# Edge rows loaded ten tiles at a time into a ring of three places, in a graph kernel that sorts its edges

## What is computed

```
edge_proj = edge_attr @ W_sum + b_sum
sum3d = segment_sum(edge_proj, src, num_segments=num_nodes)
cent_term = sigmoid(centralities @ W_cent + b_cent)
vor_term = sigmoid(voronoi_values @ W_vor + b_vor)
ref = h + z_in[in_deg] + z_out[out_deg] + cent_term + vor_term + sum3d
h = maximum(layernorm(x), 0);   result = x + ref
```

## Time and profile before

| | us |
|---|---|
| median of 3 runs | 2478.27 |
| span of the profiled execution | 3079.2 |
| POOL busy in it | 1853.9 (60%) |
| DVE busy | 1683.0 (55%) |
| PE busy | 1621.7 (53%) |
| ACT busy | 819.8 (27%) |

### The profile page before, as it was taken

The page is one execution under the profiler, slowest core; times in us unless marked ns, Lnnn a source line. Parts: engine busy times, 40 slices in busy tenths (PEclk is TensorE's granted clock), DMA queues, the critical chain, the costliest instruction groups (busy, mean ns, idle before and its releaser), DMA issues.

```text
span 3079.2 us, 40112 instructions
## 1 busy us (share of the span) xinstructions
PE 1621.7 (53%) x8689; PEld 1230.9 (40%) x8689; DVE 1683.0 (55%) x5737; ACT 819.8 (27%) x4073; POOL 1853.9 (60%) x1869
## 2 busy tenths in 40 slices
PE   5644555455555432226555554444456665568766
PEld 1223444344333320014444444333355554456655
DVE  7554456666666631346656654333455554468866
ACT  3312222232322332442232322222222222200323
POOL 5556665556565667665555655656655555556676
PEclk7756666666666655557767777767777777789988
DMA  4245433334444443334555555555556666579896
GB/s 122 85 127 151 116 106 107 99 104 122 122 121 121 126 135 106 88 107 137 155 152 164 160 160 161 143 151 148 155 156 181 183 187 178 169 189 231 210 248 187
DMA packets 485070, 451.89 MB, mean 147 GB/s; under 512 B 72407, under 2 KB 444637, under 8 KB 484828
## 3 DMA queue, kind: packets, MB, share of 16 engines
q1 hardware_dynamic: 402782, 300.08, 37.0%
q0 software_dynamic: 78752, 136.44, 14.1%
q10 hardware_dynamic: 3294, 12.80, 1.3%
HBM read 319.28 MB, written 129.59 MB: 146 GB/s over the span
## 4 chain that ended last, share of the span: by engine, by line
another core or an unknown queue 34%; DVE 19%; PE 17%; issue 15%; ACT 7%; DMA 3%; SPq 2%; POOL 2%; DVEq 1%; ACTq 0%; POOLq 0%
PE bank L1001 8%; ACT junk L864 6%; DVE hot_dh L605 3%; DVE hot_n L670 3%; DVE acc L697 2%; DVE hot_dl L605 2%; PE bank L949 2%; POOL sorted L513 2%; DMA edge_ring<-in_L_gnn_z_out_dram,out_i 2%; SPq L408 2%; DVE gate_normed L736 2%; PE bank L984 1%; PE bank L1026 1%; DVE hot_t L605 1%
## 5 line engine op out<-in xcount | busy, mean ns | idle before, releaser
L513 POOL DMA_INDIRECT sorted<-edge_ring,pos_i x1660 | 1605.8, 967 | 1103.1 <-DVE pos_i L799 633.4
L1001 PE MATMUL bank<-piece_ring,hot_n 128*125 128x129 f32 x4920 | 885.4, 336 | 260.0 <-DVE hot_n L670 209.0
L864 ACT ACTIVATE junk<-bank,mark_col 128x100 bf16<-128x100 f32 x1664 | 550.4, 343 | 1748.6 <-remote 1221.3
L1001 PEld LDWEIGHTS bank<-piece_ring,hot_n 128*125 128x125 f32 x4920 | 823.2, 241 | 367.0 <-DVE hot_n L670 248.7
L697 DVE TENSOR_TENSOR acc<-bank,acc 125x129 f32 x1230 | 352.8, 287 | 698.6 <-remote 523.9
L984 PE MATMUL bank<-hot_w,after_b 128*128 128x400 bf16 x416 | 189.3, 455 | 806.1 <-ACT junk L864 560.7
L670 DVE SCALAR_TENSOR_TENSOR hot_n<-bank,wkey,piece_ring 128x250 f32<-128x250 f32 x1230 | 579.9, 472 | 11.8 <-issue 5.2
L984 PEld LDWEIGHTS bank<-hot_w,after_b 128*128 128x128 bf16 x416 | 49.5, 119 | 866.8 <-ACT junk L864 594.3
L864 ACT ACTIVATION_READ_ACCUMULATOR junk<-bank,mark_col 128x1 f32 x1664 | 338.1, 203 | 12.3 <-issue 12.3
L605 DVE TENSOR_TENSOR hot_dl<-dst_parts,bank 128x400 bf16<-128x400 bf16 x416 | 148.0, 356 | 337.1 <-remote 305.5
L1026 PE MATMUL bank<-hot_dl,hot_dh 128*125 128x100 bf16 x1661 | 207.2, 276 | 237.4 <-DVE hot_dh L605 197.6
(11 more groups left out here) (109 smaller groups left out, 1183.2 us busy)
## 6 DMA issues: line engine op xcount, KB each, us to landing
piece_ring<-sorted SPq DMA_DIRECT2D x1230, 130.0 KB
edge_ring<-in_edge_attr_dram SPq DMA_DIRECT2D x332, 320.0 KB
sorted<-edge_ring,pos_i POOLq DMA_INDIRECT x1660
base<-in_x_dram SPq DMA_DIRECT2D x20, 560.0 KB
out_dram<-base ACTq DMA_DIRECT2D x19, 560.0 KB
out_dram<-base SPq DMA_DIRECT2D x9, 560.0 KB
base<-out_dram SPq DMA_DIRECT2D x9, 560.0 KB
edge_ring<-in_L_gnn_z_out_dram,out_i POOLq DMA_INDIRECT x100
```

Of the source, the lines that this page charges most:

```text
L513: g.indirect_dma_start(rows, bass.IndirectOffsetOnAxis(index, 0), edge_ring[:, slot, at, :], None).then_inc(s_scatter[slot], 16)
L864: last = a.activation(junk[:, t, :], part[:, t // 2, :, t % 2], ACT.Relu, bias=mark_col[:, :], accum_out=pos_f[:, q % 4, t:t + 1])
L1001: last = t_.matmul(to, hot_n[:, n % HOT_SLOTS, k, :], piece_ring[:, n % PIECE_SLOTS, k, 0:SUM], start=(k == 0), stop=(k == ROW_GROUPS[s] - 1))
```

## The change

Two numbers change:

```diff
-LOAD_TILES = 5
-EDGE_SLOTS = 6
+LOAD_TILES = 10
+EDGE_SLOTS = 3
```

## The result

The kernel with ten tiles a load took 2498.68 us, the median of 4 runs (2495.39 to 2503.53); the kernel before took 2479.23 in 4 runs beside it. The ratio is 1.0073, with a 95% interval from 1.006 to 1.0086. So the change costs 18 us by the ratio and 19.5 by these two medians. The forecast of no change (2479.5) did not come. The time lies inside the stated range (2472 to 2510) only because that range allowed for the first rival, "the smaller cushion shows" (2490, up to 2511), to which the prediction gave a chance of 0.25.

What follows compares the result with a forecast made beforehand. POOL's 1660 scatters at 1.266 us each were taken to bound the kernel, other engines running ahead; every term was 0 except 0 to 3 us on 2478.3, taken as 2479.5 us, range 2472 to 2510.

Steps and rivals of the forecast that it cites:

- the smaller cushion shows: Rival, chance 0.25: quads 25 to 31, 216, 346 outrun the cushion or quads 347 to 394 lag POOL; 5 to 33 us.
- POOL sets the pace: Whole run: 1660 scatters, one each 1.266 us, bound the kernel; the other engines run ahead; chance 0.62, with cushion sufficing.
- The tail: After the last scatter starts: 368.0 us in the profile, a little shorter in the measured runs.
- Fewer instructions, the start: ACT loses 166 row keys, SP 166 issues; longer first loads at the start stay hidden, 5 us to spare: 0 us.
- A load must wait for more of the ring: Edge ring: POOL has 20 tiles in hand, not 25; cushion falls from 24.9 to 17.0 us, still enough: 0 us.
- The load behind the third piece: Quads 347 to 394: edge load issued behind that wait costs the chain 2.1 us each; POOL loses 0 to 3 us.
- passes 5.9 us: Quads 347 to 394: the landing time of a load that decides whether the smaller-cushion rival holds.
- the prediction's own formula: Chain time per ten tiles, quads 347 to 394: 2.5q plus L + 4.5 - 2q + 0.35, quad time q, load L.
- Its own sign of being wrong: Whole run: a median over 2483 with longer ACT waits for loads, meaning a cushion under 17 us or never filled.
- Heavy quads: Quads 31, 216 and 346: making lists holds DVE 7 to 11 us over normal; the 17 us cushion covers one.
- The stops are real in the runs as well: Rival, chance 0.05: POOL waits on the chain in measured runs too, each load costs; 60 to 140 us, say 2570.
- Larger transfers help: Rival, chance 0.08 (faster): POOL's scatter issue is held up less by SP's; 8.3 us, so 2470 us.

Runs made afterwards that it cites:

- e4: Kernel before, using five of its six edge-ring places (20 tiles in hand, as in the changed kernel) with LOAD_AHEAD 3 for 4: 2481.09 us, ratio 0.9999.
- e11: Changed kernel, with half the bytes in the piece loads of quads 345 to 396, all but the first twelve: 2494.3 us, ratio 1.0047 to the kernel before.
- e2: Changed kernel, with each ten-tile edge load one quad earlier in SP's list (LOAD_AHEAD 3 for 4): 2483.59 us, ratio 1.0005 to the kernel before.
- e6: Changed kernel, with only the edge loads of quads 214 and 344 moved two quads earlier in SP's list: 2494.6 us, ratio 1.0058 to the kernel before.

## Why the prediction was right and wrong, step by step

*POOL sets the pace: right.* Step, counts and first scatter stayed. The stops of the profile of before belonged to that execution, as assumed: the new profile of before has 38.8 us of waiting for indices where the earlier trace rows have 633.4.

*The tail: right in kind, too long in the sum.* 368.0 us by the earlier trace rows, 348.4 in the new profile. The prediction saw that it had to be shorter, from 2491.7 against 2478.27.

*Fewer instructions, the start: right, 0 us.* The first scatter starts at 21.9 us in after.

*A load must wait for more of the ring: right, 0 us.* e4 takes this alone and measures 0.9999. The cushion in steady quads can be read as the time from the end of a cast to its quad's first scatter. Its median over quads 60 to 330 was 22.0 us in before, 17.6 in after and 16.5 in e4, where the sum had 24.9 for before and 17.0 for after.

*The load behind the third piece: the step that failed.* The prediction had the mechanism, the quads and the threshold ("11.7 us, while POOL takes 12.66"; "passes 5.9 us"), and put its cost at 0 to 3 us. It cost some 16.5. Three of its terms missed: two made the loop's time too short, and the cushion was taken as too full.

First, the load. It was taken at 5.0 us from issue to row key, and the median of the whole program in after is 5.1; but in quads 347 to 394 it was 6.2, from 4.8 to 7.3. Put into the prediction's own formula, with a quad of 3.85 us: 0.5 x 3.85 + 6.2 + 4.85 = 13.0 us. That alone passes 12.66. The traffic beside it explains most of it: with less of it the load took 5.4 (e11) and 5.1 (e2). By the fit in "DMA: Bandwidth & Descriptors" of the Trainium skill, anatomy of one DMA, which is for a transfer on the POOL path, an estimate is 3.5 us. The trace does not agree: it has 5.1 and 6.2. Here is what the engines did while the load of 1842.58 was under way, and behind it (columns as above; 0.94 and 0.52 are PE's granted clock, 0.96 and 0.33 the DMA share, 287 and 74 GB/s):

```profile
1842.60:1850.00 7.40, 2.84 (x25) 2.50 (x22) 5.62 (x20) 0.15 (x2) 5.11 (x6) 0.94 0.96 287
1852.10:1856.00 3.90, 3.90 (x20) 3.90 (x19) 1.65 (x7) 1.41 (x8) 2.98 (x4) 0.52 0.33 74
```

The prediction bounded the load at 3.4 and 6.8 from rows where 231 GB/s were moved, and took a value near the middle. The right stretch to price it from was the burst in which it is issued, 287 GB/s here and 278 on average over the 20 loads.

Second, the third piece. The prediction put its end 2.15 us behind the start of `rank`, by taking three fifths of the time of five pieces. The granted clock was 0.78 over its 3.85 us, so part of it ran at the higher level. But the quad that counts is the one that follows PE's wait for the load. PE in after:

```profile
1843.07 2.37 PE L1001 MATMUL bank<-piece_ring,hot_n 128*125 128x129 f32 x20
1851.42 0.51 PE L984 MATMUL bank<-hot_w,after_b 128*128 128x400 bf16 x1 [5.98 <-ACT junk L864]
...
1852.40 4.07 PE L1001 MATMUL bank<-piece_ring,hot_n 128*125 128x129 f32 x20
```

After 5.98 us without work, `rebase` takes 0.51 us in place of 0.33 and five pieces take 4.07 in place of 2.37; the granted clock is 0.52 in the row above, so the lower of its two levels (1.2 GHz). From `rank` at 1852.06 to the end of the third piece at 1852.60 + 2.59 = 1855.19 it is 3.1 us, 1.0 more than taken. So the wait makes the next load later, which makes the next wait. What the clock adds of the 13.45 us was not tried by itself. The quads between run faster than the 3.85 us taken, 2.7 from 1840.18 to 1842.90, and that gives back part. In all, issue to row key is 6.04 us on average over the 19 intervals, 1.0 more than taken, and the rest of the loop is 7.41 us in place of 0.5 x 3.85 + 4.85 = 6.78, so 0.6 more: 11.78 + 1.04 + 0.63 = 13.45.

Third, the cushion at the entry. The prediction let 15 us of it absorb the loss in these quads. But quads 343 to 345 empty it: the index of quad 342 was ready 21.7 us ahead of POOL, that of quad 345 0.3 us. SP's list at the start of the last segment in after:

```profile
1748.75 0.39 SPq L421 DMA_DIRECT2D edge_ring<-in_edge_attr_dram  x1
1761.93 6.02 SPq L408 DMA_DIRECT2D piece_ring<-sorted  x10
1768.01 0.42 SPq L421 DMA_DIRECT2D edge_ring<-in_edge_attr_dram  x1
1768.62 22.08 SPq L408 DMA_DIRECT2D piece_ring<-sorted  x15
1790.76 0.42 SPq L421 DMA_DIRECT2D edge_ring<-in_edge_attr_dram  x1
```

Before the first piece of a sorted segment, SP waits until all of its tiles are scattered (12.2 us in after, 11.9 in before), then issues ten piece loads in one go, and only then the edge load: 1768.01 - 1748.75 = 19.3 us between two edge loads, and 22.8 us to the next. In before there are five piece loads ahead of the first edge load and five between it and the next:

```profile
1758.80 2.89 SPq L408 DMA_DIRECT2D piece_ring<-sorted  x5
1761.74 0.42 SPq L421 DMA_DIRECT2D edge_ring<-in_edge_attr_dram  x1
1762.36 2.87 SPq L408 DMA_DIRECT2D piece_ring<-sorted  x5
1765.28 0.43 SPq L421 DMA_DIRECT2D edge_ring<-in_edge_attr_dram  x1
```

At quad 345 the index was ready 4.8 us ahead of POOL's first scatter in before and 0.3 us in after. Before then gains on POOL and is at 12 us by quad 350. After stays between 0.3 and 4.4 us up to quad 396. The place of the edge load is the smaller part of this: with the load moved ahead of SP's wait (e6) the index of quad 345 is ready 4.1 us ahead, and in e2, which loses nothing, 1.6. The wait for the whole segment stands in all of these runs; only a loop slower than POOL fails to fill the cushion again behind it. So nothing was left to absorb 20 x (13.45 - 12.66) = 16 us, and 16.5 were measured. The sum of the prediction had this loss at 18 us in its worst case and took 15 off for the cushion. Its own sign of being wrong named this: a median over 2483, since the cushion was smaller "or never filled".

*Heavy quads, taken as covered: 4 us too small.* Around quad 216 POOL waited 5.3 - 1.2 = 4.1 us longer than in before, and no longer once the load of quad 214 was moved (e6). The rest of quads 217 to 339 cost nothing, as predicted: the first scatter of quad 235 starts 3.9 us later than in before, that of quad 340 3.5. The 4.1 us were of the same kind as at quad 345: an edge load late in SP's list at a segment's start.

*The rivals.* "The smaller cushion shows" gave the right sign, with the chain of quads 347 to 394 as one of its two legs. That leg was priced at 9 us and cost 16.5. Of the other, up to 8 us at each of three places, the one at quad 216 came by itself, with 4.1 us, and e4 shows that fewer tiles in hand weren't its cause. So the size came right because one leg was too small and the other too large, which is luck. "The stops are real in the runs as well" fell: the new profile has 38.8 us of waiting for indices. Its price was also added up wrongly, since 20 x 2.1 us and 1 to 2 us on 50 others are 92 to 142 us and not 60 to 140. "Larger transfers help" fell: POOL's mean of 966 ns is as before, and with the place mended (e2) larger loads give 1.0005. "Perfetto Trace Analysis" of the Trainium skill calls them the first remedy when DMA-bound. The traces here show no gain from them: POOL's scatters set the pace of before.

## What to carry to other kernels

When a transfer is made larger, look not only at how many bytes the ring holds, but at what stands ahead of it in its queue: a load that waits on the work it feeds closes a loop, and the loop's time is what counts against the pace of the slowest engine. Price the transfer from the stretch in which it is issued, which its place in the queue also decides, and the engine's work right behind a wait at the speed it has there. A cushion counts only as full as it is where the slow stretch begins; look for the wait on a whole stage that empties it.

## What was not expected of the hardware

The time of a 640 KB load depended on its neighbours nearly as much as on its size. From issue to row key the median is 3.8 us for 320 KB in before and 5.1 for 640 KB in after. In quads 347 to 394 of after it is 6.2; it is 5.4 there when the piece loads had half their bytes, and 5.1 when the load stood one quad earlier.

One profiled execution of the kernel before had a span of 3079.2 us and another of 2482.7, on the same instructions; ACT's stops of 1221.3 us for "remote" were in the first alone.
